# Registers in the middle of each chunk of keys, values kept per column tile and loaded three chunks at a time

## The reference

```
qkv = gn(x) @ qkv_w.T + qkv_b            # 12 heads of 32 channels
reg_k, reg_v = registers @ qkv_w[384:].T + qkv_b[384:]    # 16 registers
scores = q . [k, reg_k] / sqrt(32)       # a position sees its 7x7 window (clamped at the edges)
attn   = softmax(scores)                 #   and all 16 registers
o      = attn @ [v, reg_v];   x = x + o @ out_w.T + out_b
```

## Time and profile before

| | |
|---|---|
| three runs | 669.73, 671.38, 671.67 us |
| profiled execution | 672.79 us, its span 671.0 us |
| TensorE matmuls busy | 585.5 us (87%) |
| VectorE busy | 474.6 us (71%) |
| ScalarE busy | 301.7 us (45%) |
| GpSimd busy | 281.9 us (42%) |
| mean granted TensorE clock | 0.974 of full speed |
| DMA | 95.44 MB, mean 142 GB/s |

### The profile page before, as it was taken

How to read it: one execution, slowest core, us unless ns; L and a number is a source line. 1 busy time by engine, 2 the same in 40 slices (tenths; PEclk the granted TensorE clock), 3 DMA queues, 4 the chain that set the end, 5 groups by cost and what they waited for, 6 DMA issues and landing times.

```text
span 671.0 us, 22415 instructions
## 1 busy us (share of the span) xinstructions
PE 585.5 (87%) x9227; PEld 408.7 (61%) x9227; DVE 474.6 (71%) x1033; ACT 301.7 (45%) x597; POOL 281.9 (42%) x421
## 2 busy tenths in 40 slices
PE   3578799998989988998899988889888789997997
PEld 3337676677756766567675867557666445564554
DVE  5885575777967799785866868858798786772232
ACT  1861554224623488313552256331774428544221
POOL 3116896262222745337982632115646122212131
PEclk9998999998999999999999999979998899998999
DMA  9769675996268751687419944397630001110112
GB/s 298 189 147 292 189 204 144 222 263 156 56 147 205 222 138 44 166 226 202 129 48 251 256 135 129 73 240 203 172 93 21 1 32 39 58 51 35 72 49 93
DMA packets 131565, 95.44 MB, mean 142 GB/s; under 512 B 67292, under 2 KB 125320, under 8 KB 131464
## 3 DMA queue, kind: packets, MB, share of 16 engines
q1 hardware_dynamic: 121960, 75.18, 43.4%
q0 software_dynamic: 9504, 18.84, 9.0%
HBM read 57.62 MB, written 35.54 MB: 139 GB/s over the span
## 4 chain that ended last, share of the span: by engine, by line
PE 54%; DVE 19%; DMA 8%; SPq 7%; issue 5%; ACT 4%; POOL 2%; ACTq 0%; DVEq 0%; POOLq 0%
PE ps L1052 39%; PE ps L1215 5%; PE ps L1166 5%; SPq L272 4%; DVE MX L555 4%; DMA KB<-kscr 3%; PE ps L1192 2%; DVE ST L448 2%; DMA vscr<-VT 2%; DVE GT_ L487 2%; DVE SUMT L568 1%; DMA kscr<-KT 1%; SPq L255 1%; DVE KT L525 1%; DVE RINV L574 1%
## 5 line engine op out<-in xcount | busy, mean ns | idle before, releaser
L555 DVE TENSOR_REDUCE MX<-ps 128x2 f32<-128x456 f32 x216 | 125.5, 626 | 47.0 <-PE ps L1166 45.9
L1052 PE MATMUL ps<-XH,WQ 128*128 128x384 f16 x810 | 145.2, 334 | 9.6 <-DVE XH L497 7.7
L1052 PEld LDWEIGHTS ps<-XH,WQ 128*128 128x128 f16 x810 | 79.1, 100 | 66.3 <-ACT XH L818 7.6
L877 ACT ACTIVATE PT<-ps 128x448 f32<-128x448 f32 (+1 forms) x162 | 78.6, 510 | 58.1 <-PE ps L1192 57.3
L1166 PE MATMUL ps<-KB,QS 120*32 120x228 f16 x1728 | 66.8, 272 | 20.8 <-DVE MX L555 9.6
L427 POOL TENSOR_TENSOR KT<-QS,KT 128x384 f16<-128x384 f32 x36 | 32.7, 918 | 107.9 <-ACT KT L966 107.9
L1192 PE MATMUL ps<-QS,KB 122*128 122x112 f16 (+1 forms) x864 | 64.6, 214 | 10.7 <-ACT PT L877 5.9
L1052 PE MATMUL ps<-WQ,XH 128*128 128x128 f16 x972 | 61.2, 220 | 4.3 <-issue 4.0
L374 POOL DMA_DIRECT2D QS<-MT x72 | 38.2, 535 | 59.8 <-ACT MT L867 59.7
L1215 PE MATMUL ps<-PT,VR 128*32 128x112 f32 (+1 forms) x1296 | 61.0, 262 | 2.6 <-DMA VR<-vscr 2.2
L1192 PEld LDWEIGHTS ps<-QS,KB 122*128 122x128 f16 x864 | 43.8, 100 | 31.6 <-ACT PT L877 14.8
(11 more groups left out here) (167 smaller groups left out, 1004.5 us busy)
## 6 DMA issues: line engine op xcount, KB each, us to landing
KB<-kscr SPq DMA_DIRECT2D x108, 192.0 KB, 6.9
kscr<-KT SPq DMA_DIRECT2D x72, 192.0 KB, 2.5
VR<-vscr SPq DMA_DIRECT2D x216, 56.0 KB
QS<-qscr SPq DMA_DIRECT2D x108, 96.0 KB, 5.9
out<-X SPq DMA_DIRECT2D x12, 576.0 KB, 3.3
X<-in_x SPq DMA_DIRECT2D x6, 576.0 KB, 7.2
qscr<-QT POOLq DMA_DIRECT2D x18, 192.0 KB, 3.6
qscr<-PT POOLq DMA_DIRECT2D x18, 192.0 KB, 5.1
```

The source lines that it names most:

```text
L555: V.tensor_reduce(out=MX[:, s % 2, t, 2 * pair:2 * pair + 2], in_=ps[:, S_BANK(s, i), 0:2 * RUN].rearrange("p (h n) -> p h n", h=2), op=AL ...
L877: A(PTS[n % 4][:, 0:w], ps[:, ST_BANK(n), 0:w], ACT.Exp, scale=SCORE).then_inc(s_["exd"], 1)
L1052: last = mm(bank, lhsT(a, k), rhs(b, k), start=(k == 0 and n == 0), stop=(finish and k == steps - 1 and n == 2))
```

## The change

1. The registers move from the end of each chunk of keys to its middle, after the first 4 rows: 56 keys, 16 registers, 56 keys. A block of 32 queries is 4 rows, so the run it needs is now 42 + 56 + 16 + 42 = 156 columns, and starts at one of two places of the chunk. The mask tables, the padding and the register positions in `KT` and `VR` follow. The copies of `keys_low` keep their number and size and write to two pieces of 56 a chunk.
2. `vscr` is stored per column tile, with all 14 columns that the tile needs. `values_out` still writes 8 columns a tile; the 3 columns on each side are copied from one tile's area of DRAM to its neighbour's by new DMAs in SyncE's queue (`borders`): 10 a stage, 48 rows of 1536 B each.
3. `values_in` waits for these copies (`b_out`) and issues 4 DMAs a tile in place of 6: 3 chunks of one half (56 partitions) each. The first three chunks of a tile are loaded when `weighted` has passed the third chunk of tile `s - 2`, the rest when it has passed the sixth.
4. In the last stage the loads of the second layer's weights stand after the values of tile 3.
5. In stages 2 and 5 `group_sums` and `group_copy` come after the second strip of keys, and `group_means` after the fifth.
6. The warm-up at the start has 36 matmuls on 42 rows in place of 26 on 58.

```diff
-LEAD, TAIL = 3 * KW + REGS, 3 * KW
-SLOTW = LEAD + STRIPS * CHUNK + TAIL
-RUN = LEAD + CHUNK + TAIL
+HALO = 3 * KW
+HALF = 4 * KW
+SLOTW = 2 * HALO + STRIPS * CHUNK + REGS
+RUN = 2 * HALO + HALF + REGS
-WARM = 26
+WARM = 36
-        vscr = nc.dram_tensor("vscr", [H, PADW, P], F32, kind="Internal").ap()
+        vscr = nc.dram_tensor("vscr", [TILES, H, KW, P], F32, kind="Internal").ap()
...
+            def borders(gi, t):
+                for e in (t,) if True else [2 * b + t // 3 for b in range(KC)]:
+                    sp.wait_ge(v_out[e], 48 * (gi + 1))
+                if t:
+                    sp.dma_start(vscr[t - 1, :, 3 + CT_:KW, :], vscr[t, :, 3:6, :]).then_inc(b_out[t - 1], 16)
+                if t < TILES - 1:
+                    sp.dma_start(vscr[t + 1, :, 0:3, :], vscr[t, :, CT_:CT_ + 3, :]).then_inc(b_out[t + 1], 16)
+
             def values_in(gi, s):
-                for t in {s, min(s + 1, TILES - 1)}:
-                    sp.wait_ge(v_out[t], 48 * (gi + 1))
-                if 36 * gi + 6 * (s - 1) > 0:
-                    sp.wait_ge(s_["pv"], 36 * gi + 6 * (s - 1))
+                sp.wait_ge(b_out[s], (32 if 0 < s < TILES - 1 else 16) * (gi + 1))
...
-                for a in range(STRIPS):
-                    sp.dma_start(VR[0:8 * KW, s % 2, a, :], vscr[8 * a:8 * a + 8, CT_ * s:CT_ * s + KW, :]).then_inc(vr_in[s % 2][a // 3], 16)
-
+                for a in (0, 3):
+                    if 36 * gi + 6 * (s - 2) + a + 3 > 0:
+                        sp.wait_ge(s_["pv"], 36 * gi + 6 * (s - 2) + a + 3)
+                    for half in range(2):
+                        rows = vscr[s, 8 * a:8 * a + 24].rearrange("(a h r) c n -> h (r c) a n", h=2, r=4)
+                        sp.dma_start(VR[half * (HALF + REGS):half * (HALF + REGS) + HALF, s % 2, a:a + 3, :], rows[half]
+                                     ).then_inc(vr_in[s % 2][a // 3], 16)
...
+                borders(gi, 0)
                 for s in (0, 1):
+                    borders(gi, s + 1)
                     values_in(gi, s)
-                if gi == STAGES - 1:
...
                     if s < 2:
                         sp.wait_ge(s_["st_mm"], 36 * gi + 6 * (s + 1))
                         keys_in(gi, s + 4)
+                    if s < 3:
+                        borders(gi, s + 3)
                     values_in(gi, s + 2)
+                    if gi == STAGES - 1 and s == 1:
+                        for i in (0, 5):
+                            sp.wait_ge(v_out[i], 48 * STAGES)
+                        for src, dst in ((fc2, f2raw), (rw, rwraw)):
+                            sp.dma_start(dst, src).then_inc(s_["f_in"], 16)
...
@@ keys_low
-                    last = V.tensor_copy(KT[:, a % 3, part, :, 0:8 * KW].rearrange("p s (r c) -> p s r c", c=KW), windows(a, part))
+                    to = KT[:, a % 3, part, :, :]
+                    parts = bass.AP(to.tensor, to.offset, [list(to.ap[0]), [CHUNK, TILES], [HALF + REGS, 2], [KW, 4], [1, KW]])
+                    last = V.tensor_copy(parts, windows(a, part))
@@ vector, after keys_low(gi, a)
+                        if gi in (2, 5) and a == 1:
+                            group_copy(gi // KC + 1, 0)
@@ scores
-                        a, q0 = 2 * t + j // 2, s * SN + 128 * t + 32 * j
+                        at, q0 = CHUNK * (2 * t + j // 2) + j % 2 * HALF, s * SN + 128 * t + 32 * j
...
-                                  KB[0:SROWS, h, slot(s), CHUNK * a:CHUNK * a + RUN], start=True, stop=True)
+                                  KB[0:SROWS, h, slot(s), at:at + RUN], start=True, stop=True)
@@ tensor, after keys(gi, a)
+                    if gi in (2, 5) and a == 1:
+                        pe.wait_ge(s_["kr_lo"], KC)
+                        pe.wait_ge(s_["mx"], 36 * gi)
+                        pe.wait_ge(s_["t_ev"], 6 * gi)
+                        group_sums(gi // KC + 1, 0)
+                    if gi in (2, 5) and a == 4:
+                        group_means(gi // KC + 1, 0)
```

More of the change, by code:

```diff
@@ L184, in build @@
         v_out = [sem(f"v_out{i}") for i in range(TILES)]
+        b_out = [sem(f"b_out{i}") for i in range(TILES)]
         q_out = [sem(f"q_out{i}") for i in range(TILES)]
@@ L305, in _ @@
                         keys_in(gi, s + 4)
+                    if s < 3:
+                        borders(gi, s + 3)
                     values_in(gi, s + 2)
+                    if gi == STAGES - 1 and s == 1:
[3 more added lines that the diff above has]
+                            sp.dma_start(dst, src).then_inc(s_["f_in"], 16)
+                        for j in range(3):
+                            sp.dma_start(b2raw[DH * j:DH * j + EXPERTS, :], fb2).then_inc(s_["b2_in"], 16)
+                        sp.dma_start(PICK[0:96, :], pick).then_inc(s_["moe_in"], 16)
             sp.wait_ge(s_["st_mm"], 36 * STAGES)
@@ L329, in _ @@
             pool.wait_ge(s_["zeros"], 1)
-            for side in (0, W + 3):
-                pool.dma_start(vscr[:, side:side + 3, :], SUMT[0:H, :]).then_inc(s_["vpad"], 16)
+            for tile, side in ((0, 0), (TILES - 1, 3 + CT_)):
+                pool.dma_start(vscr[tile, :, side:side + 3, :], SUMT[0:H, :]).then_inc(s_["vpad"], 16)
             def low_half(n, blk, k):
@@ L344, in register_keys @@
                     for part in range(2):
-                        last = nc.gpsimd.tensor_copy(KT[:, i, part, :, CHUNK - REGS:CHUNK],
+                        last = nc.gpsimd.tensor_copy(KT[:, i, part, :, HALF:HALF + REGS],
                                                      KR[:, part, gi % KC, :].unsqueeze(1).broadcast_to([P, TILES, REGS]))
@@ L1438, in key_tables @@
     for a in range(STRIPS):
-        at = LEAD + CHUNK * a
+        row = [HALO + CHUNK * a + KW * r + r // 4 * REGS for r in range(8)]
+        registers = slice(row[4] - REGS, row[4])
         for q in range(max(0, 8 * a - 8), min(H, 8 * a + 16)):
@@ L1442, in key_tables @@
                 if first(q, H) <= 8 * a + r < first(q, H) + WIN:
[L1443 removed]
+                    out[:, q % 16, row[r]:row[r] + KW] = 0
             if q // 8 == a:
[L1445 removed]
+                out[:, q % 16, registers] = 0
         for kind, s in enumerate((0, 2, TILES - 1)):
@@ L1450, in key_tables @@
                     if f <= X0[s] + i < f + WIN:
-                        out[kind, 16 + c, at + i:at + 8 * KW:KW] = 0
-                out[kind, 16 + c, at + 8 * KW:at + CHUNK] = 0
+                        out[kind, 16 + c, [at + i for at in row]] = 0
+                out[kind, 16 + c, registers] = 0
     return out
```

36 lines of the change are left out of this document (9 added, 27 removed).

## The result

The kernel after took 686.53 us (median of 4 runs, 684.85 to 688.79) against 671.52 us for the kernel before (4 runs, 669.73 to 672.15). The ratio is 1.0219, with a 95% interval of 1.0177 to 1.0262: slower by 15 us. The forecast was 664.4 us with a range to 681, so the time lies outside it. Rival (b), the copies queueing, had given 688. The profiled execution took 688.79 us, its span is 687.0 us, its mean granted TensorE clock 0.959 (before 0.974).

The account below looks back on a forecast made before the run. In the tile loop SyncE's queue sets the pace, TensorE and VectorE close behind. Stages -0.5 and group sums -6.5 give -7.0 on the profiled 672.8, so 665.8, or 664.4 us on the median's scale; range 651 to 681.

Parts of the forecast that it names:

- Rival (b): SyncE's queue: border copies queue behind the loads around them and loads issue slower; +17 us, 688 us, chance 0.19.
- -0.5 for all the rest: Stages 0 to 5 without group sums: -2, -1.5, -0.8, +0.5, +0.8 and +2.5 us, together -0.5 us.
- Rival (a): SyncE's queue: new loads issue in 0.47 us and copies land fast; 17 us faster in all, 654 us, chance 0.17.
- point of decision: SyncE's queue: the change loses from about 1.5 us more a stage than counted, through slower copies and load issues.
- expected gains of stages 0 and 1: Stages 0 and 1: shorter TensorE work comes through and delayed keys are absorbed or not late; -2 and -1.5 us.
- Late weights: Last stage: fc2 loads behind tile 3's values make ScalarE stand 7 us; +6 us, stage at +2.5.
- rival (d): TensorE: score matmuls don't get shorter because of a floor; only stages 0 and 2 feel it; 667 us, chance 0.04.
- the +12 held for them: Keys' phase: if key copies took twice as long, 72 x 0.34 us, half on the path, +12 us.
- rival (c): Gains cancel: ScalarE's stand in the last stage costs 10 us with a TensorE clock fall, stages lose 2; 671, chance 0.13.

Follow-up runs that it names:

- early copies: Each border copy issued one load of values earlier in SyncE's queue, on the kernel after, all work kept: 667.70 us, 0.9943 of the kernel before.
- early weights: Loads of fc2 and the router's weights issued before the last stage's border copies, on the kernel after: 681.94 us, 1.0139 of the kernel before.
- without waits: On the kernel after, border copies written to a DRAM tensor nobody reads, no load waiting for them, border columns zero: 665.52 us, 0.9921 of the kernel before.

## Why the prediction was wrong

**The budget.** From the ratios: group sums -4.8 us, the new layout without its copies -7, issue and traffic of the copies +7, the waits for them +20. The sum is the measured +15 us by construction, as each term is the step from one kernel to the next. The forecast had about -6.5 for the group sums and -0.5 for all the rest.

**The step that failed is the size of B and, above all, of B'**, the time from the issue of a copy to its landing, B' behind a fresh load of keys. I took 2.4 us, and 3.1 behind keys, from L247, which writes more than twice the bytes out of SBUF. Of the copies that a load waits for, the two a stage ahead of the keys of tile 4 took 2.7 us in the middle of all twelve (2.2 to 4.0, and once 8.2), the two behind keys 4.2 (2.8 to 5.6). The pauses are then 2 x 2.7 + 2 x 4.2 = 13.8 us a stage where I had 11.0. If all of it lay on the path, that is 17 us over six stages, an estimate, of the 24.7 us by which the stages together missed (+17.7 for -7.0).

Why B' is longer, the runs show: the same copy took 4.5 to 4.6 us behind the keys of tile 4 and 2.5 to 2.9 ahead of them. Four loads of 84 KB ahead of a copy did much less, 2.5 us in the middle for the copy between tile 0's and tile 1's values. The rows of before had a sign of a long tail that I used only as an end of the range: the landing of L247 reaches 4.8 us.

The Trainium skill, "DMA: Bandwidth & Descriptors", section "Anatomy of one DMA", gave an estimate of 2.2 us for it. The section fits its figures to DMAs issued from GpSimd, which the prediction did not say; these went out from SyncE. The shortest copy of the kernel after took 2.2 us, and the usual one 1.2 us more, so the measurement decides against it.

**How it adds up in stage 3.** The forecast had the keys of tile 4 at 9.4 us after the landing of tile 1's values. Measured 12.0 us (315.97 to 328.00): B 3.7 + 4.0 against 4.8, and the eight loads 1.71 + 2.55 us with their gaps, 4.4, against 4.6. Keys of tile 5: forecast 5.4 us after, measured 6.5 (329.66 to 336.20). Values of tile 3: B' 4.5 against 3.1. The sum, 5 us later than forecast by tile 3, stands against a stage 3 that came out 3.6 us worse than forecast (+4.1 for +0.5). In stages 1, 2, 4 and 5 the same interval reads 11.0, 10.3, 8.5 and 12.3 us, where the kernel before had 8.5, 8.5, 8.5 and 11.6.

**p**, the issue of a load, was taken as 0.58 us with its gap. The median is 409 ns and the gap 40. In stage 3 the four loads took 1.71, 2.55 and 2.65 us, so 0.43 to 0.67 each: long ones among them ate the difference. Rival (a) needed the quick issue and had it in the median; it failed on its own B of 2.0 and B' of 2.7. Rival (b) was nearly right in B 2.9 and B' 4.5 and wrong in p 0.69, so that 688 us came out near 686.5 is in part luck. Its point of decision was 1.5 us a stage; B up by 0.3 and p up by 0.06 make 4 x 0.3 + 14 x 0.06 = 2.0 us, not 1.5, and the pauses alone were 2.8 us longer.

**The expected gains of stages 0 and 1** did not come: +5.0 and +3.8 us instead of -2 and -1.5. In stage 0 I had put no copy on the path: for the keys of tile 4 with a reason, for those of tile 5 with none. The chain of the kernel after there:

```profile
66.64 2.88 issue
...
80.17 5.85 DMA KB<-kscr
...
89.12 4.22 DMA KB<-kscr
```

The stall ahead of the first weighted sums stands in the kernel without copies too (2.88 us at 66.36), so it is not from them; the first sums came 1.35 us late with it. The copy ahead of tile 0's values took 8.2 us and yet cost nothing that shows: the kernel without copies started its first weighted sums only 0.6 us earlier (76.14 against 76.73). The copy behind the keys of tile 4 did cost: it took 5.6 us (from 80.64), and the keys of tile 5 were issued 4.2 us later than before (87.94 against 83.79). With early copies the stage is 1.8 us late, not 5.0.

In stage 1, the stretch from the end of stage 0's weighted sums to the first scores is 1.8 us longer, ahead of every copy (29.4 against 27.6), and in the kernel with group sums alone 2.5 us longer; that part is not from the new layout alone and I have no cause for it.

**Late weights.** ScalarE stood 5.84 us (forecast 7), and the last stage lost. The mechanism is in the trace; for the size, +6 us, the run with early weights has 5 +- 5, which does not settle it. What I had not seen is that it depends on the pauses.

**Group sums**: -6.5 forecast, -4.8 +- 2.2 measured. This is TensorE of the kernel after in stage 2, where there was 2.13 us of idle time before the second row:

```profile
198.70 0.35 PE L1076 MATMUL ps<-SM,GD 128*32 128x2 f32 x6 [1.61 <-DVE KR L526]
...
203.47 0.82 PE L1082 MATMUL ps<-GM,GU 32*128 32x2 f32 x6
```

The wait for the group copy is gone; 1.61 us of it came back a strip earlier as a wait for the register keys L526, which the prediction had seen and put at about a microsecond, to be absorbed.

**Right in size**: maxima 478 ns (476), though the bounds of 20 to 40 us for their gain should have been 29 to 43 by their own working (measured 31). A unit of eight score matmuls takes 135 ns from start to start where it took 195 (forecast 140), and the score matmuls together are busy 55.3 us where they were 66.8, so rival (d), the floor, falls. Key copies are unchanged at 344 ns (341 before), so the +12 held for them was not needed.

**The clock** fell in the last stage, which the prediction had only in rival (c). Windows of the kernel after in the last stage (us, then busy time of each engine with its count, granted clock, DMA share, GB/s):

```profile
470.00:475.00 5.00, 1.60 (x31) 1.46 (x33) 1.30 (x5) 0.49 (x1) 3.15 (x6) 0.92 1.08 260
475.00:480.00 5.00, 5.00 (x78) 4.38 (x78) 1.93 (x5) 0.49 (x1) 0.28 (x1) 0.50 0.71 220
...
505.00:510.00 5.00, 1.59 (x60) 1.05 (x57) 4.14 (x8) 0.54 (x2) 2.82 (x4) 0.83 0.54 144
510.00:515.00 5.00, 1.48 (x24) 1.08 (x28) 0.00 (x0) 3.62 (x8) 0.91 (x1) 0.50 0.50 150
```

Twice TensorE was busy for only a third of 5 us, and then had its lower level, 1.2 GHz (0.50). So these idle stretches were paid once as idle and once more in slower work behind them. How much that is of the 15 us stays open. Over 61 runs of the kernel before, a straight line gives 203 us for a whole unit of mean clock (correlation -0.47), and 0.974 less 0.959 would then be 3 us. The kernel with group sums has 0.982 in the median and is 4.8 us faster for a reason of its own, so a mean clock does not separate cause from effect.

## What to carry to other kernels

A DMA that a later DMA waits for cost its latency once for each such pair here, as both were issued back to back from one in-order queue. With the queue's other work put between them, the same copies cost next to nothing: of 20 us of waits 1.5 +- 3.6 were left. Price such a latency by what stands ahead of it in the queue, here 2.7 us or 4.2 us behind a load of keys, and not from the median of another transfer. Before crediting shorter work on an engine, see what sets the pace in that stretch: 30 us of saved maxima were worth 5 +- 3 us at best. And time each part of a change by itself: the one part that paid here, the group sums, had nothing to do with the layout.

## What the runs showed of the hardware

- A copy of 72 KB from DRAM to DRAM took 2.2 us at least, 3.3 to 3.5 in the middle and 8.7 at most from issue to landing in the kernel after, longer than 192 KB from SBUF to DRAM (2.5 in the middle). From ScalarE's queue it was 2.7 and 3.2 in the middle.
- The cost of an issue went by the shape more than by the bytes here. The old load of 8 x 14 rows onto 112 partitions took 648 ns, the new one of 56 partitions in three pieces, with half as many bytes again, took 409:

```profile
L283 SPq DMA_DIRECT2D VR<-vscr x144: 307/409/2098, 72.4 to 520.8; - x144
```

- TensorE stood for "issue", that is for nothing that the profile shows, far longer than before (there 4.0 us at L1052 and 1.2 at L1166). The waits of TensorE in the kernel after:

```profile
PE ps L1183 <- issue: 10.5, 5, 3.4
...
PE ps L1232 <- issue: 6.3, 4, 2.3
...
PE ps L1069 <- issue: 3.5, 2, 2.7
```

Of the eleven such stalls over 0.6 us in the kernel after, ten end 1.4 to 1.7 us after a packet of the instruction queue (q8 on the page) has ended, which suggests late instructions behind busy DMA engines and does not show it. All kernels with the new layout have more of it than the kernel before, those without copies or without waits too (9.4 us at the score matmuls with no copies). The longest, 3.4 us, is the one ahead of the first fall of the clock above. So part of what the layout should have given may be lost here. No run isolates it, and its cause stays open.
